# Turning a unit's row maxima by one fp16 matmul of pre-split parts instead of one fp32 matmul

## The chip, the cores and the metric

The kernel runs on one core of a Trainium2 chip. The metric is the device time of one execution in microseconds (us). The kernel before takes 2337.19 us, the median of three runs (2336.58 to 2337.27).

## The reference, cut to what matters

One transformer layer with attention and a feed-forward part side by side on the same normalised input: `x + attention(xn) + ffn(xn)`, for x of 2 x 1024 x 1024. What the change touches is the softmax of the attention:

```python
scores = jnp.einsum('bhqd,bhkd->bhqk', q, k) / np.sqrt(HEAD_DIM)   # 32 heads of 32 channels, 8 key heads
attn = jax.nn.softmax(scores, axis=-1)
out = jnp.einsum('bhqk,bhkd->bhqd', attn, v)
```

A softmax needs the maximum of each row of scores, which is taken off before the exponential.

## The kernel before, in words

The work has three stages: the projections to queries, keys and values (to about 236 us), attention (to about 1030 us), and the output projection with the feed-forward part. Every instruction is written out in Python, so each engine has one fixed order.

Attention goes over 32 units (one of 16 key-head and batch pairs, times two halves of the queries) of 16 steps each, 512 steps in all. In a unit there are 16 row tiles of 128 query rows. The scores are made twice. `row_scores` (L1448) makes them with queries on the partitions, into three PSUM banks in turn, and `row_max` (L1131) on VectorE reduces each bank of 512 columns to a maximum; this runs LEAD = 25 steps ahead. `key_scores` (L1501) makes them again with keys on the partitions, with two extra contraction rows that take off the row maximum; ScalarE takes the exponential (L809). `values` (L1515) multiplies by the values in fp32, GpSimd adds pairs of probability tiles (L649), and `pair_sums` (L1530) sums them by a matmul of ones in fp32.

TensorE runs `row_scores`, `key_scores`, `values` and `pair_sums` as sets of four matmuls, each with 32 columns of weights, in four column groups of the array (output partitions 0 to 31, 32 to 63, and so on). The set of an instruction raises its semaphore with its last matmul.

The maxima of a unit lie in `mxs` with the row's place on the partition and the tile on the column. They must become rows of `qst`, along the free dimension. The way there, for unit u + 1, in steps 6 to 8 of unit u:

- step 6: VectorE does the last `row_max` of unit u + 1, then `top_max` (L1135), which merges the two halves into `mtop` (128 x 16, fp32), and raises `top_ok`.
- step 7: TensorE, after its four score sets of this step, waits for `top_ok` and does `maxima_rows` (L1456): the fp32 matmul of `mtop` with the unit matrix into 16 partitions of bank 7. VectorE, after the two `row_max` of this step, does `split_rows` (L1140 and L1142): scale to a high fp16 part, then the rest as a low fp16 part, from PSUM, and raises `mrow_ok`.
- step 8: SyncE's queue sends the two parts to rows 96 and 97 of `qst` (`load_m`, L393). TensorE's first `pair_sums` of the unit (step 8) waits for `mrow_ok`, since it writes the same bank.

`row_scores` of set c waits in `max_ok` for the reduction of set c - 3, since there are three banks. On VectorE `settle()` makes the next instruction wait until the one before it has written.

Of the kernel before, what the change touches and what calls it, by code (L numbers as in the profile page):

```python
# [5 lines left out]
P = 128  # L6
# [14 lines left out]
MU = 16384.0  # L21
# [115 lines left out]
def layer_kernel(nc, x, wq, sq, wk, sk, wv, sv, wo, so, gw, gz, gs, uw, uz, us, dw, dz, ds, out, zscr, wscr, yscr, kscr, vscr, rscr):  # L137
    f32, f16, i32 = mybir.dt.float32, mybir.dt.float16, mybir.dt.int32
    ALU = mybir.AluOpType
    ACT = mybir.ActivationFunctionType  # L140
    AX = mybir.AxisListType.X
    add, sub, mult, amin, amax, iseq = ALU.add, ALU.subtract, ALU.mult, ALU.min, ALU.max, ALU.is_equal

    ctx = ExitStack()
    with ctx:
# [52 lines left out]
        zone_d = zone_b[:, 74 * 256:75 * 256]  # L198
        mxs = zone_d[:, 0:64].rearrange("p (n h c) -> p n h c", n=2, h=2)
        mtop = zone_d[:, 64:80]  # L200
        ones = zone_d[:, 80:112]
        dcp = zone_d[:, 112:144].rearrange("p (n c) -> p n c", n=2)

        woT = view(zone_b, 20, 4096, f16).rearrange("p (k c) -> p k c", k=FQ)
        woraw = [view(zone_b, kb, 1024) for kb in (0, 12, 44, 48, 52, 12, 44, 8)]
# [29 lines left out]
        id32 = sb("id32", [P, P])  # L235
        id16 = sb("id16", [P, P], f16)
        zone_c = sb("zone_c", [P, 768])
        bn = zone_c[:, 0:NX * 12].rearrange("p (n c) -> p n c", n=NX)
        mask = zone_c[:, 256:768]
        mrow = zone_c[0:16, 0:256].bitcast(f16).rearrange("p (n h c) -> p n h c", n=2, h=2)  # L240
        tab = zone_c[:, 0:IT * 16].rearrange("p (t m g) -> p t m g", t=IT, m=2)
        dtab = zone_c[:, IT * 16:IT * 24].rearrange("p (t o) -> p t o", t=IT)
        cmx = zone_c[:, IT * 24:IT * 26].rearrange("p (t m) -> p t m", t=IT)
# [19 lines left out]
        ps = ctx.enter_context(nc.psum_tensor("ps", [P, 8, 512], f32))  # L263
# [35 lines left out]
        s = {n: sem(n) for n in names}  # L299
# [40 lines left out]
        def _(sp):  # L340
# [49 lines left out]
            def load_m(u):  # L390
                sp.wait_ge(s["mrow_ok"], u + 1)
                for part in range(2):
                    sp.dma_start(qst[u % 3][96 + part:97 + part, :, :].rearrange("a h (q c) -> a (h q) c", q=4),  # L393
                                 mrow[:, u % 2, part, :]).then_inc(s[f"m_in{u % 3}"], 16)

            def store_kv(b):
                sp.dma_start(kscr[2 * b:2 * b + 2].rearrange("n h p c -> p n h c"), kz[:, 2 * b:2 * b + 2, :, :]
# [57 lines left out]
            for e in range(STEPS):  # L455
                u, k = e // 16, e % 16
# [509 lines left out]
        def _(dve):  # L966
            V = nc.vector
            ch = Tally(s["chain"])

            def settle():  # L970

                dve.wait_ge(s["chain"], ch.value())
# [159 lines left out]

            def top_max(u):
                dve.wait_ge(s["max_ok"], 32 * u + 32)
                V.tensor_reduce(mtop, mxs[:, u % 2, :, :].rearrange("p h c -> p c h"), AX, amax).then_inc(s["top_ok"], 1)  # L1135

            def split_rows(u):
                dve.wait_ge(s["m_pe"], u + 1)
                m = ps[0:16, 7, 0:P]
                ch.inc(V.tensor_scalar(mrow[:, u % 2, 0, :], m, -1.0 / MU, None, mult))  # L1140
                settle()
                V.scalar_tensor_tensor(mrow[:, u % 2, 1, :], m, -1.0 / MU, mrow[:, u % 2, 0, :], mult, sub).then_inc(s["mrow_ok"], 1)  # L1142

            def invert(u):
                dve.wait_ge(s[f"dc_in{u % 2}"], 64 * (u // 2 + 1))
# [3 lines left out]
            for c in range(NC):  # L1149
                i = 4 * (c + 1)  # L1150
                for p in range(12):
                    if c + 1 < NC:
                        if p == 0:
                            dve.wait_ge(s[f"x_in{c + 1}"], 64)
                            moments((i, i + 1))
                        elif p == 1:
                            if c == 0:
                                guard_output(0, 1)
                            moments((i + 2, i + 3))
                            statistics(c + 1)  # L1160
                        elif p == 2:
                            inverse_deviation(c + 1)
                            normalise((i, i + 1))
                        elif p == 3:
                            normalise((i + 2, i + 3))
                        elif c == 0 and p == 4:
                            low(i)
                        elif (7 if c == 0 else 6) <= p < 10:
                            low(i + p - 6)
                    for r in early_row(c, p, 0) + early_row(c, p, 1):  # L1170
                        row_max(r)
                        if r == 15:
                            top_max(0)
                    if (c, p) == (3, 9):
                        split_rows(0)
                    if (c, p) == (NC - 1, 11):
                        break
                    if (c, p) != (0, 1):
                        guard_output(c, p)
                    if (c, p) in ((0, 5), (0, 9)):  # L1180
                        place_weights(9 if p == 5 else 11)
                    if (c, p) == (0, 8):
                        negate_zeros()
                    if p >= 3:
                        tail(c, p - 1)
                if c + 1 < NC:
                    tail(c, 11)
# [106 lines left out]
            for e in range(STEPS):  # L1294
                u, k = e // 16, e % 16
                if e + LEAD < STEPS:
                    row_max(e + LEAD)
                if e == 0:
                    clamp_output(NC - 1, 11)
                elif e == 2:  # L1300
                    keep_numbers(NC - 1, 11)
                elif e in (5, 7):
                    tail(NC - 1, 10 + (e - 5) // 2)
                if k == 6 and u + 1 < UNITS:
                    top_max(u + 1)
                if k == 7 and u + 1 < UNITS:
                    split_rows(u + 1)
                if u == UNITS - 2 and k == 9:
                    table_sizes()
                if u == UNITS - 2 and k == 10:  # L1310
                    common_maxima()
                if k == 10 and u:
                    invert(u - 1)
                if u == UNITS - 2 and k == 11:
                    common_product()
                    ch.inc(V.tensor_scalar(fac[:, 2:3], cmr[:, 2:3], 256.0 * 1024.0 / QB, None, mult))
                    settle()
                if u == UNITS - 1:
                    if k == 2:
                        output_magnitude(0)  # L1320
                    elif k == 8:
                        output_magnitude(1)
                        output_scales(0)
                    elif k == 9:
                        evac_output_weights(0)
                    if by_vector(u, 1) and k % 4 == 3:
                        add_pair(u, k // 4, 1)
# [80 lines left out]
        def _(pe):  # L1408
            MM = nc.tensor.matmul
# [42 lines left out]
            def maxima_rows(u):  # L1452
                pe.wait_ge(s["top_ok"], u + 1)
                if u >= 2:
                    pe.wait_ge(s["evd_ok"], u - 1)
                MM(ps[0:16, 7, 0:P], mtop, id32[:], start=True, stop=True).then_inc(s["m_pe"], 1)  # L1456

            def project(c, p):
                n, b2, s2, f = 12 * c + p, c // 2, c % 2, channels(c, p)
# [145 lines left out]
            for e in range(STEPS):  # L1605
                u, k = e // 16, e % 16
# [104 lines left out]
            for hf in range(HALVES):  # L1711
                for j in range(PAIRS):
                    if hf == 1 and j in TURNS:
                        n = 2 * TURNS.index(j)
# [43 lines left out]
```

## Time and profile before

| what | value |
|---|---|
| median of the runs | 2337.19 us (2336.58 to 2337.27) |
| span of the profiled execution | 2335.8 us |
| TensorE busy, share of the span | 98% |
| VectorE / ScalarE / GpSimd busy | 77% / 68% / 42% |
| granted TensorE clock, mean | 0.997 of full speed |
| row maxima: `top_max` | 32 of 188 ns |
| row maxima: matmul | 64 halves of 272 ns |
| row maxima: `split_rows` | 32 of 269 ns and 32 of 279 ns |

The span goes from the first to the last instruction of the profiled execution; no separate time of that execution is given. Its span is 0.8 us under the fastest and 1.4 us under the median of the runs. Busy time of TensorE is modelled at the ends of matmuls, so starts of instructions say more than ends. In a timeline the columns are the start, the length, the engine, the line, the operation, the tiles and the count; several instructions of one line are merged, and brackets give idle time before them with what ended it. PEld is the weight load of TensorE.

### The profile page before, as it was taken

To read this page: it belongs to the slowest core of one execution; us is meant where nothing else is said; L and a number is where in the kernel's file an instruction comes from. 1 tells how busy PE (TensorE), PEld (TensorE's weight loads), DVE (VectorE), ACT (ScalarE), POOL (GpSimd) and SP (SyncE) were. 2 spreads that over 40 slices of the span, in tenths; PEclk is the share of its full clock that TensorE was granted. 3 is DMA by queue.
4 is the path that set the end of the run, shared out by engine and by line. 5 is a ranking of instruction groups with operands and counts; after the bars stand their busy time and mean duration, and the time that the engine had idled before them with its cause. 6 is when DMAs were issued, how large, how long until landed. Compare 5 with 4: busy or idle time off the path is not lost.

```text
span 2335.8 us, 44834 instructions
## 1 busy us (share of the span) xinstructions
PE 2284.4 (98%) x18443; PEld 1100.0 (47%) x18443; DVE 1809.7 (77%) x2313; ACT 1591.0 (68%) x2051; POOL 990.0 (42%) x559
## 2 busy tenths in 40 slices
PE   6999999999999999999999999999999999999998
PEld 3444455555555555534444444444444444444444
DVE  8878888888888888856677777777777777777777
ACT  6774788888888888872366666666665666666664
POOL 0450699999999999960022222210002222221000
PEclk9999999999999999999999999999999999999999
DMA  5891344444444444443111111121114111114111
GB/s 187 171 202 32 70 72 78 74 76 70 72 81 72 74 72 73 80 92 136 59 37 36 44 47 37 36 109 45 37 64 145 36 36 37 38 53 181 36 36 72
DMA packets 178305, 175.51 MB, mean 75 GB/s; under 512 B 87778, under 2 KB 127586, under 8 KB 178102
## 3 DMA queue, kind: packets, MB, share of 16 engines
q1 hardware_dynamic: 113590, 143.28, 19.5%
q0 software_dynamic: 64512, 29.37, 12.6%
q8 instruction: 146, 2.39, 0.4%
q14 instruction: 57, 0.47, 0.1%
HBM read 160.08 MB, written 65.45 MB: 97 GB/s over the span
## 4 chain that ended last, share of the span: by engine, by line
PE 90%; DVE 5%; ACT 2%; issue 1%; DMA 1%; SPq 0%; POOL 0%; DVEq 0%; ACTq 0%
PE ps L1676 33%; PE ps L1692 17%; PE ps L1448 9%; PE ps L1501 9%; PE ps L1515 9%; PE ps L1647 5%; PE ps L1530 4%; PE ps L1473 3%; DVE sm L977 1%; DVE zone L1112 1%; DVE zone L1016 1%; ACT zone L809 0%; ACT zone L741 0%; ACT zone L789 0%; DVE zone L1388 0%
## 5 line engine op out<-in xcount | busy, mean ns | idle before, releaser
L1676 PE MATMUL ps<-xT,zone 128*128 128x512 f16 x3584 | 774.6, 379 | 2.7 <-DVE zone L1388 2.7
L1131 DVE TENSOR_REDUCE zone<-ps 128x1 f32<-128x512 f32 x1024 | 639.1, 683 | 128.1 <-PE ps L1448 120.0
L809 ACT ACTIVATE zone<-ps,sm 128x512 f32<-128x512 f32 x1024 | 628.8, 693 | 115.3 <-PE ps L1501 110.9
L649 POOL TENSOR_TENSOR zone<-zone 128x1024 f32<-128x1024 f32 x252 | 619.1, 2543 | 123.9 <-ACT zone L809 70.0
L1365 DVE TENSOR_SCALAR ps<-ps,zone_c 128x1024 f32<-128x1024 f32 x392 | 506.7, 1293 | 160.5 <-PE ps L1676 158.5
L932 ACT ACTIVATE ps<-ps,zone_c 128x1024 f32<-128x1024 f32 x392 | 426.7, 1088 | 259.9 <-PE ps L1676 259.9
L1676 PEld LDWEIGHTS ps<-xT,zone 128*128 128x128 f16 x3584 | 350.3, 98 | 426.2 <-DVE zone L1388 4.2
L1448 PE MATMUL ps<-zone 96*32 96x512 f16 (+1 forms) x3946 | 437.3, 380 | 8.6 <-issue 3.6
L1501 PE MATMUL ps<-zone 98*32 98x512 f16 x4096 | 438.3, 381 | 4.5 <-ACT zone L809 4.2
L1692 PE MATMUL ps<-zone 128*128 128x512 f16 x1792 | 387.1, 379 | 0.0
L684 POOL CAST zone<-zone 128x1024 f16<-128x1024 f32 x56 | 58.1, 1037 | 692.2 <-DVE zone L1369 692.2
L1376 DVE TENSOR_SCALAR ps<-ps,zone_c 128x1024 f32<-128x1024 f32 x216 | 279.2, 1293 | 93.1 <-PE ps L1692 92.9
L946 ACT ACTIVATE ps<-ps,zone_c 128x1024 f32<-128x1024 f32 x216 | 235.1, 1088 | 137.8 <-PE ps L1692 137.8
L1515 PE MATMUL ps<-zone 128*32 128x512 f32 x2048 | 278.8, 594 | 0.7 <-ACT zone L809 0.7
L1692 PEld LDWEIGHTS ps<-zone 128*128 128x128 f16 x1792 | 175.3, 98 | 211.4
L1448 PEld LDWEIGHTS ps<-zone 96*32 96x32 f16 (+1 forms) x3946 | 145.8, 96 | 160.4 <-issue 65.7
L1501 PEld LDWEIGHTS ps<-zone 98*32 98x32 f16 x4096 | 145.5, 96 | 147.7 <-issue 71.7
L1473 PE MATMUL ps<-xT,zone 128*128 128x512 f16 x768 | 176.7, 384 | 1.0 <-DVE xT L1038 1.0
L692 POOL TENSOR_TENSOR xT<-xT,zone 128x1024 f32<-128x1024 f32 x8 | 18.7, 2358 | 361.8 <-ACT zone L951 361.8
L1530 PE MATMUL ps<-zone 128*32 128x512 f32 x1024 | 141.4, 595 | 0.0
L686 POOL TENSOR_TENSOR zone<-zone 128x1024 f16<-128x1024 f32 x56 | 119.1, 2127 | 4.5
L1473 PEld LDWEIGHTS ps<-xT,zone 128*128 128x128 f16 x768 | 74.9, 99 | 89.1 <-issue 5.9
(138 smaller groups left out, 1387.6 us busy)
## 6 DMA issues: line engine op xcount, KB each, us to landing
zone<-dequantised SPq DMA_DIRECT2D x84, 512.0 KB, 3.6
dequantised<-zero_points SPq DMA_DIRECT2D x56, 256.0 KB, 4.0
zone<-zone SPq DMA_DIRECT2D x384, 32.0 KB, 2.3
zone<-_attn_hidden_states_dram SPq DMA_DIRECT2D x16, 512.0 KB, 6.6
zone<-inverse_sums SPq DMA_DIRECT2D x128, 64.0 KB, 2.0
attention<-zone SPq DMA_DIRECT2D x32, 256.0 KB, 2.0
xT<-attention SPq DMA_DIRECT2D x4, 2048.0 KB, 12.2
dequantised<-zero_points POOLq DMA_DIRECT2D x28, 256.0 KB, 11.2
```

Of the source, the lines that this page charges most:

```text
L649: nc.gpsimd.tensor_tensor(duo[n % 3], prob[:, prob_slot(e), :], prob[:, prob_slot(e + 2), :], add).then_inc(s["sum_ok"], 1)
L809: A(prob[:, prob_slot(e), m % 2 * 512:(m % 2 + 1) * 512], ps[:, 3 + m % 3, :], ACT.Exp, scale=gam[:, 0:1]).then_inc(s["exp_ok"], 1)
L932: A(pair, pair, ACT.Copy, scale=tab[:, t, 0, g:g + 1]).then_inc(s["act_ok"], 1)
L1131: V.tensor_reduce(mxs[:, u % 2, half, i % 16:i % 16 + 1], ps[:, (2 * i + half) % 3, :], AX, amax).then_inc(s["max_ok"], 1)
L1365: V.tensor_scalar(pair, pair, tab[:, t, 1, g:g + 1], None, mult).then_inc(s["dve_ok"], 1)
L1376: V.tensor_scalar(pair, pair, dtab[:, it, o:o + 1], None, mult).then_inc(s["dve_ok"], 1)
L1448: last = MM(ps[a:a + wide, c % 3, :], qst[u % 3][0:96, i % 16 // 4, c0:c0 + wide], kst[0:96, u // 2 % 2, half * 512:(half + 1) * 512], sta ...
L1473: last = MM(ps[:, output_bank(n), :], wT[:, kt, f * P:(f + 1) * P], xT[:, b2, part, kt, s2 * 512:(s2 + 1) * 512], start=(kt == 0 and part ...
L1501: last = MM(ps[32 * b:32 * b + 32, 3 + m % 3, :], kst[0:98, u // 2 % 2, kt * P + 32 * b:kt * P + 32 * b + 32], qst[u % 3][0:98, 2 * hp + a ...
L1515: last = MM(ps[32 * h:32 * h + 32, 6, :], vst[:, u // 2 % 2, kt, :], prob[:, prob_slot(2 * kt + h // 2), h % 2 * 512:(h % 2 + 1) * 512], s ...
L1676: last = MM(ps[:, 4 * s2 + 2 * m + c, :], ring[:, buf, m * H + g * P:m * H + (g + 1) * P], xT[:, hf, part, g, c * 512:(c + 1) * 512], star ...
L1692: last = MM(ps[:, 4 * s2 + 2 * m + c, :], ring[:, k % RING, (it % 4) * 512 + o * P:(it % 4) * 512 + (o + 1) * P], hT[:, it, part, c * 512: ...
```

## The change

The scaling and the split move ahead of the turn. `top_max` now reduces, waits for the write, scales to the high part in fp16, waits again, and makes the low part, into `mparts` (128 x 32, fp16); only then it raises `top_ok`. It has a new wait for the earlier `maxima_rows`. The matmul takes the 32 columns of `mparts` as fp16 weights and the fp16 unit matrix. `split_rows` becomes `place_rows`, one copy of 32 partitions from PSUM to `mrow`. The two DMAs are as before, from other partitions.

```diff
+        mparts = zone_d[:, 144:160].bitcast(f16)
...
-        mrow = zone_c[0:16, 0:256].bitcast(f16).rearrange("p (n h c) -> p n h c", n=2, h=2)
+        mrow = zone_c[0:32, 0:128].bitcast(f16).rearrange("p (n c) -> p n c", n=2)
...
-                                 mrow[:, u % 2, part, :]).then_inc(s[f"m_in{u % 3}"], 16)
+                                 mrow[16 * part:16 * part + 16, u % 2, :]).then_inc(s[f"m_in{u % 3}"], 16)
...
             def top_max(u):
                 dve.wait_ge(s["max_ok"], 32 * u + 32)
-                V.tensor_reduce(mtop, mxs[:, u % 2, :, :].rearrange("p h c -> p c h"), AX, amax).then_inc(s["top_ok"], 1)
-
-            def split_rows(u):
+                ch.inc(V.tensor_reduce(mtop, mxs[:, u % 2, :, :].rearrange("p h c -> p c h"), AX, amax))
+                settle()
+                if u:
+                    dve.wait_ge(s["m_pe"], u)
+                ch.inc(V.tensor_scalar(mparts[:, 0:16], mtop, -1.0 / MU, None, mult))
+                settle()
+                V.scalar_tensor_tensor(mparts[:, 16:32], mtop, -1.0 / MU, mparts[:, 0:16], mult, sub).then_inc(s["top_ok"], 1)
+
+            def place_rows(u):
                 dve.wait_ge(s["m_pe"], u + 1)
-                m = ps[0:16, 7, 0:P]
-                ch.inc(V.tensor_scalar(mrow[:, u % 2, 0, :], m, -1.0 / MU, None, mult))
-                settle()
-                V.scalar_tensor_tensor(mrow[:, u % 2, 1, :], m, -1.0 / MU, mrow[:, u % 2, 0, :], mult, sub).then_inc(s["mrow_ok"], 1)
+                V.tensor_copy(mrow[:, u % 2, :], ps[0:32, 7, 0:P]).then_inc(s["mrow_ok"], 1)
...
-                MM(ps[0:16, 7, 0:P], mtop, id32[:], start=True, stop=True).then_inc(s["m_pe"], 1)
+                MM(ps[0:32, 7, 0:P], mparts, id16[:], start=True, stop=True).then_inc(s["m_pe"], 1)
```

`split_rows` is replaced by `place_rows` at both places where it was called.

## Rows read from the trace of the kernel before

**Rows 1.** The page, busy time of each engine (share of the span) and instructions

```profile
PE 2284.4 (98%) x18443; PEld 1100.0 (47%) x18443; DVE 1809.7 (77%) x2313; ACT 1591.0 (68%) x2051; POOL 990.0 (42%) x559
```

**Rows 2.** Groups of instructions by shape: busy us, mean ns | idle before, releaser

```profile
L1456 PE MATMUL ps<-id,zone 128*16 128x128 f32 x64 | 12.3, 272 | 0.2 <-DVE zone L1135 0.2
...
L1142 DVE SCALAR_TENSOR_TENSOR zone_c<-ps,zone_c 16x128 f16<-16x128 f32 x32 | 8.9, 279 | 1.1
...
L1140 DVE TENSOR_SCALAR zone_c<-ps 16x128 f16<-16x128 f32 x32 | 8.6, 269 | 0.5 <-PE ps L1456 0.5
...
L1135 DVE TENSOR_REDUCE zone<-zone 128x16 f32<-128x32 f32 x32 | 6.0, 188 | 1.1
```

**Rows 3.** Timeline of TensorE's matmuls around one turn, 472.9 to 479.6 us

```profile
472.95 0.41 PE L1448 MATMUL ps<-zone 96*32 96x512 f16 x4
...
476.46 0.38 PE L1456 MATMUL ps<-id,zone 128*16 128x128 f32 x2
...
476.90 0.38 PE L1501 MATMUL ps<-zone 98*32 98x512 f16 x1
477.12 0.38 PE L1448 MATMUL ps<-zone 96*32 96x512 f16 x1
477.19 0.53 PE L1501 MATMUL ps<-zone 98*32 98x512 f16 x4
...
478.27 1.16 PE L1530 MATMUL ps<-zone 128*32 128x512 f32 x8
479.13 0.52 PE L1448 MATMUL ps<-zone 96*32 96x512 f16 x4
```

**Rows 4.** Timeline of TensorE's weight loads around the same turn

```profile
476.84 0.15 PEld L1448 LDWEIGHTS ps<-zone 96*32 96x32 f16 x4
477.18 0.10 PEld L1501 LDWEIGHTS ps<-zone 98*32 98x32 f16 x4 [0.18 <-ACT zone L809]
...
478.11 0.41 PEld L1530 LDWEIGHTS ps<-zone 128*32 128x32 f32 x8 [0.45 <-issue]
```

**Rows 5.** Timeline of VectorE around the same turn, and the next turn's start

```profile
473.42 2.48 DVE L1131 TENSOR_REDUCE zone<-ps 128x1 f32<-128x512 f32 x4 [0.98 <-PE ps L1448]
475.94 0.19 DVE L1135 TENSOR_REDUCE zone<-zone 128x16 f32<-128x32 f32 x1
476.10 1.29 DVE L1131 TENSOR_REDUCE zone<-ps 128x1 f32<-128x512 f32 x2
...
477.81 1.27 DVE L1131 TENSOR_REDUCE zone<-ps 128x1 f32<-128x512 f32 x2
479.71 2.48 DVE L1131 TENSOR_REDUCE zone<-ps 128x1 f32<-128x512 f32 x4 [0.63 <-PE ps L1448]
...
500.48 0.19 DVE L1135 TENSOR_REDUCE zone<-zone 128x16 f32<-128x32 f32 x1
```

**Rows 6.** Timeline of VectorE in the statistics of the input, 96.3 to 99.8 us

```profile
96.95 0.16 DVE L993 TENSOR_SCALAR sm<-sm 128x4 f32<-128x4 f32 x1
97.03 0.16 DVE L994 TENSOR_SCALAR sm<-sm 128x4 f32<-128x4 f32 x1
...
98.89 0.16 DVE L1006 TENSOR_TENSOR sm<-sm 128x4 f32<-128x4 f32 x1
99.08 0.17 DVE L1008 TENSOR_SCALAR sm<-sm 128x4 f32<-128x4 f32 x1
```

**Rows 7.** Groups of instructions by shape: small VectorE instructions

```profile
L1209 DVE COPY zone_c<-ps 128x224 f32<-128x224 f32 x1 | 0.6, 578 | 0.0
...
L1254 DVE SCALAR_TENSOR_TENSOR zone_c<-sm,zone_c 128x28 f32<-128x28 f32 x1 | 0.2, 209 | 0.0
```

**Rows 8.** Timeline of VectorE at a turn with a stall behind it

```profile
600.62 1.29 DVE L1131 TENSOR_REDUCE zone<-ps 128x1 f32<-128x512 f32 x2 [1.80 <-PE ps L1448]
```

**Rows 9.** Timeline of weight loads at the turn that starts at 252.15 us

```profile
254.92 0.54 PEld L1530 LDWEIGHTS ps<-zone 128*32 128x32 f32 x8 [1.17 <-issue]
```

**Rows 10.** Timeline of weight loads at the last turn, 995.86 us

```profile
996.52 0.10 PEld L1501 LDWEIGHTS ps<-zone 98*32 98x32 f16 x4 [0.25 <-ACT zone L809]
```

More of the change, by code:

```diff
@@ L1174, in _ @@
                     if (c, p) == (3, 9):
-                        split_rows(0)
+                        place_rows(0)
                     if (c, p) == (NC - 1, 11):
@@ L1306, in _ @@
                 if k == 7 and u + 1 < UNITS:
-                    split_rows(u + 1)
+                    place_rows(u + 1)
                 if u == UNITS - 2 and k == 9:
```

## The prediction, made before the changed kernel was seen

> **What bounds the kernel now.** I read the page first. TensorE is busy 98% of the span, VectorE 77% [rows 1]; so a change pays or costs only where it moves TensorE. Then the groups of instructions by shape, for the price of what is removed [rows 2], and last the timelines of one turn of the maxima, engine by engine, because the change moves work of 0.1 us between engines and only an order in time tells who waits.
>
> The turn comes once a unit, and a unit takes 24.54 us (from 475.94 to 500.48) [rows 5]. On TensorE the four score matmuls of a set run in four column groups at once. The turn of 16 columns uses the first group alone: its two halves sit there for two steps of 0.11 us, while the other groups go on with the next set. So after the turn the first group is 0.22 us behind. One sees it in the rows: the four-matmul rows are 0.41 us long ahead of the turn and 0.52 us long after it, and the first group's last score matmul of the step stands alone at 477.12 [rows 3]. The late group counts: in the undisturbed place VectorE starts its reduction 0.47 us behind the first matmul of the set (472.95 to 473.42), after the turn 0.58 us (479.13 to 479.71) [rows 3, 5]. The semaphore comes when the slowest group is done. The other groups use their lead only to stand at the next wait for an exponential (477.18) [rows 4]. So the first group sets the pace of the unit, and it is where I count.
>
> **What is removed on TensorE.** Two halves of an fp32 matmul, 0.22 us of the first group per turn. One fp16 pass of 128 columns comes in; fp16 score matmuls of 512 columns follow each other in the first group after 0.22 us (476.90 to 477.12) [rows 3], so 128 columns are about 0.055 us. Gain: 0.165 us a turn, if nothing else waits.
>
> **What is added on VectorE, ahead of the signal.** `top_ok` used to fire at the end of one reduction of 0.19 us [rows 2]. Now two small instructions and two waits stand ahead of it. A small tensor-scalar takes 0.16 to 0.17 us on 4 columns [rows 6], say 0.175 on 16. The low part is a scalar-tensor-tensor: 0.209 us on 28 columns [rows 7], 0.279 on 128 columns from PSUM [rows 2]; at about 1 ns a column this leaves 0.16 to 0.20 on 16 columns, and I take 0.17, nearer to the shape that has its fp16 output. A waited start comes 0.035 us behind the end of the one before: 98.89 plus 0.16 to 99.08 [rows 6]. The chain is 0.19 + 0.035 + 0.175 + 0.035 + 0.17 = 0.605 us.
>
> VectorE starts the next, independent instruction 0.03 us ahead of the end of the last (475.94 plus 0.19 against 476.10) [rows 5]. The next `row_max` therefore starts at 475.94 + 0.605 - 0.03 = 476.515 instead of 476.10.
>
> **What waits for that.** `top_ok` itself arrives at about 476.60, and the weight load of the turn was wanted at 476.24. The turn's matmul starts at about 476.65 instead of 476.46, but is 0.165 shorter, so the set behind it starts at 476.70 against 476.68: this wait alone just eats the gain.
>
> Behind it is a second wait, and it is the one that decides. The second score set after the turn needs the bank that this `row_max` empties. Today it starts at 476.10, and the weights of that set load at 476.84, 0.74 us later [rows 4, 5], which is the reduction and the signal; the first group takes it at 477.12 anyway [rows 3]. With the `row_max` at 476.515 the release comes at 477.26 and the matmuls of all four groups start at 477.27 to 477.30. That is 0.15 to 0.18 us behind 477.12; a weight load that had to wait costs about 0.01 more. I take +0.165 us a turn for the group that sets the pace. From here to the next turn that group had nothing to spare: the exponentials and banks that it needs are there before it is ready for them (477.18 against 477.33, 0.22 behind 477.12), so the loss stays.
>
> Bounds of this step. Shortest: both instructions 0.155 and 0.16, the waits 0.03: the chain is 0.535, and the loss 0.09 us. Longest: 0.20 and 0.23, and 0.05 for the wait that now has two semaphores: 0.74 in all, and the loss 0.30 us.
>
> **What is taken off VectorE after the signal.** `split_rows` was 0.27 + 0.035 + 0.28 us [rows 2]; `place_rows` is one copy of 128 columns from PSUM, about 0.27. VectorE is 0.415 late into the step and gives 0.3 back, and it stood idle 0.63 us ahead of 479.71 [rows 5], which covers the rest; without this cover the next reductions would be 0.1 us late. `mrow_ok` came at 477.89 (0.19 + 0.28 ahead of the `row_max` at 477.81, which overlaps by 0.07). It now comes when two `row_max` of 0.605 us and the copy are done: 476.515 + 1.21 + 0.27 = 478.00. The pair sums wait for it; their weights load 0.22 us after it today (478.11) [rows 4]. With 478.22 that is well ahead of the new start of 478.58 (478.27 today [rows 3], plus 0.31 for the three groups that lose their lead). The two DMAs of step 8 start 0.1 us later, and the unit's key scores need them six steps, some 9 us, later. SyncE's queue behind them next wants step 11. POOL waits for the pair sums, and moves with TensorE. The new wait for the last unit's turn is 24 us old when it is asked.
>
> **The sum over the turns.** Of the 31 turns in the loop, 24 look like the one shown, with the `row_max` 0.16 us behind `top_max` and the turn's matmul at 0.52.
> - 24 x 0.165 = +4.0 us.
> - Four turns have a stall of TensorE on the queries and keys right ahead (VectorE idle 1.53, 1.80, 0.67 and 1.88 us, at 351.72, 598.63, 796.96 and 895.81); one of them is shown [rows 8]. There VectorE has finished the chain before TensorE asks, and the shorter matmul counts: 4 x -0.16 = -0.6 us.
> - The turn at 674.09 has a short stall (`row_max` 0.31 behind); gain and loss cancel: 0.
> - The turn at 252.15 lies in a stretch where VectorE is the late one and TensorE's pair sums wait for `mrow_ok` (1.17 us idle) [rows 9]. There the whole growth of VectorE's work counts: 0.415 + 0.27 - 0.585 = +0.1, with a margin +0.2.
> - The turn at 995.86 has no `row_max` behind it, and the next exponential ends TensorE's wait anyway [rows 10]: 0.
> - The turn of unit 0 is in the projections, long after its maxima are ready: -0.16.
>
> Together +3.4 us. The profiled span of 2335.8 becomes 2339.2; the median of the runs lies 1.4 above the span, so 2340.6 us, +0.15%.
>
> **A rule weighed.** The rows have two small instructions start 0.08 us apart without a wait (96.95, 97.03) and 0.19 us apart with one (98.89, 99.08) [rows 6], and the chain of 0.605 us is made of the second kind. The Trainium skill, "VectorE: DVE Perf Modes", section "The DRAIN you can't avoid", says that an operation waits for the pipeline to empty anyway and that the semaphore costs nothing extra. By that rule the two kinds would be alike; the rows differ by 0.11 us. What a cheap wait would give is the third rival.
>
> **The rivals.**
> - *TensorE keeps its gain.* If the chain on VectorE were hidden, each turn would save 0.165 us: 31 x -0.165 = -5.1, 2332.1 us. It decides when the `row_max` behind the chain starts by 476.20, a chain of at most 0.29 us; up to 476.36 there is still some gain. For it speaks that TensorE is at 98% and this is pure TensorE work. Against it, three small instructions with waits between them in the rows never come near 0.29.
> - *The two cancel.* Only the wait for `top_ok` counts and the bank's release does not bind, because the groups take the set in another order than I read: 24 x 0, less 0.8 in the special turns, 2336.4 us. For it: the release (476.84) lies close to where the set would load anyway, and may be dispatch and not the semaphore.
> - *The waits are cheap.* If a wait on the instruction just ahead cost no more than the 0.08 us of an unwaited start, the chain would be 0.08 + 0.08 + 0.19 = 0.35 us, the `row_max` would start at 476.26 and the second set at 477.01: 24 x -0.11 - 0.8 = -3.4, 2333.8 us. The skill's rule named above speaks for it; 32 waited pairs of the old split, 0.31 us apart for 0.27 us of work, speak against it.
> - *The pair sums wait for the copy.* If `place_rows` is slow, `mrow_ok` binds too. A copy from PSUM took 0.578 us for 224 columns [rows 7]; at that rate 128 columns would be 0.33 to 0.39. Then `mrow_ok` comes at 478.12, still 0.2 us short of binding. It takes a copy above 0.6 us; then the loss would be some 0.4 us a turn, 24 x 0.4 = +9.6, 2346.8 us.
> - *The stalls on the queries move.* The four stalls and the short one make about 7 us in all. They hang on how transfers lie to each other, and a unit that is 0.2 us longer could shift them by up to their sum either way: from 2333.6 to 2347.6 with the rest as forecast. They hold in part for the other cases too.
>
> **How the numbers follow.** What a measurement of this kernel can tell from no change is about 0.2%, 4.7 us, so from 2332.5 to 2341.9 us is the same. My forecast, the bank's release, gets 0.64. Its own range is 24 x 0.09 - 0.8 = +1.4 to 24 x 0.30 - 0.6 = +6.6, 2338.6 to 2343.8 us; 0.40 of it lies within 0.2% and 0.24 above. TensorE keeps its gain: 0.08, faster. The two cancel: 0.11, same. The waits are cheap: 0.05, same. The pair sums wait: 0.08, slower. Moved stalls: 0.04, half faster, half slower. Faster is 0.10, same 0.56, slower 0.34. The range goes from the cheap waits to the far end of the forecast with a little for the stalls, 2333.6 to 2344.5 us; what is left out, 0.20, is the kept gain, the pair sums and the moved stalls.
>
> **What the changed profile would show.** In a turn like the one shown: `row_max` 0.58 us behind the reduction of `top_max` (0.16 today); the turn's matmul at 0.70 (0.52); four-matmul rows of 0.41 us on both sides of the turn, since no group is behind; the second score set at 1.33 to 1.36 us in all groups (1.18 in the first today), with its weight load released by VectorE; a unit of 24.70 us (24.54). In the turns with a stall, that stretch is 0.16 us shorter. I am wrong if the `row_max` is later or earlier than 0.55 to 0.71, if the second score set doesn't follow it by 0.75, or if the unit's length doesn't follow that set.

## The result, and the profile after

The changed kernel takes 2440.13 us (median of four runs, 2438.49 to 2445.97) against 2336.89 (four runs, 2336.35 to 2337.27) of the kernel before on the same chip: a ratio of 1.0444, 95% interval 1.0431 to 1.0457. That is 103 us slower where the prediction said 3.4. The profiled execution has a span of 2436.7 us against 2335.8.

The page of the changed kernel, busy time by engine, and the end of its chain by engine:

```profile
PE 2300.7 (94%) x18411; PEld 1021.0 (42%) x18411; DVE 1900.2 (78%) x2345; ACT 1595.2 (65%) x2051; POOL 987.6 (41%) x559
PE 83%; DVE 12%; ACT 2%; issue 1%; DMA 0%; SPq 0%; DVEq 0%; POOL 0%; ACTq 0%
```

VectorE has 90.5 us more of busy time (1809.7 before [rows 1]). The groups by shape say which instructions hold it; behind the bar are the busy time, the mean ns of one, and the idle time ahead with its releaser:

```profile
L1142 DVE SCALAR_TENSOR_TENSOR zone<-zone 128x16 f16<-128x16 f32 x32 | 53.7, 1677 | 1.1
L1140 DVE TENSOR_SCALAR zone<-zone 128x16 f16<-128x16 f32 x32 | 47.9, 1498 | 1.1
L1146 DVE CAST zone_c<-ps 32x128 f16<-32x128 f32 x32 | 8.6, 269 | 0.3 <-PE ps L1460 0.3
L1136 DVE TENSOR_REDUCE zone<-zone 128x16 f32<-128x32 f32 x32 | 6.0, 187 | 1.1
L1460 PE MATMUL ps<-id,zone 128*32 128x128 f16 x32 | 7.5, 235 | 84.2 <-DVE zone L1142 84.2
```

The two new instructions on 16 columns were priced at 0.175 and 0.17 us. They take 1.50 and 1.68 us in the mean, 101.6 us together, of which 32 x 0.345 = 11 was foreseen. The reduction (L1136) and the copy (L1146) cost what was foreseen. TensorE waits 84.2 us for them at the turn (L1460), in 30 of the 32 turns.

One plain turn, VectorE, GpSimd and TensorE in the timelines (start, length, instruction; it is the tenth turn, the one of [rows 3, 5] is the eleventh):

```profile
471.72 0.19 DVE L1136 TENSOR_REDUCE zone<-zone 128x16 f32<-128x32 f32 x1
471.94 0.82 DVE L1140 TENSOR_SCALAR zone<-zone 128x16 f16<-128x16 f32 x1
472.80 2.27 DVE L1142 SCALAR_TENSOR_TENSOR zone<-zone 128x16 f16<-128x16 f32 x1
474.98 1.27 DVE L1132 TENSOR_REDUCE zone<-ps 128x1 f32<-128x512 f32 x2
```

```profile
471.46 1.27 POOL L654 TENSOR_TENSOR zone<-zone 128x512 f32<-128x512 f32 x1
472.69 2.33 POOL L650 TENSOR_TENSOR zone<-zone 128x1024 f32<-128x1024 f32 x1
```

```profile
472.60 0.40 PE L1505 MATMUL ps<-zone 98*32 98x512 f16 x4
475.12 0.23 PE L1460 MATMUL ps<-id,zone 128*32 128x128 f16 x1 [2.11 <-DVE zone L1142]
475.12 0.44 PE L1452 MATMUL ps<-zone 96*32 96x512 f16 x4
```

```profile
475.72 0.10 PEld L1452 LDWEIGHTS ps<-zone 96*32 96x32 f16 x4 [0.43 <-DVE zone L1132]
```

Read the ends. The tensor-scalar starts while GpSimd's divide (L654, a product with the inverted sums) runs and ends at 472.76, 0.03 us behind the divide's end at 472.73. The scalar-tensor-tensor starts 0.11 us into GpSimd's pair add (L650) and ends at 475.07, 0.05 behind the add's end at 475.02 on these rounded numbers. The end of each is set by an engine with which it shares no data. The first wait makes the second: it brings VectorE to the start of the next add, and so into its whole length. `row_max` (L1132), which empties the bank for TensorE, starts 3.26 us behind the merge, where it was 0.16 [rows 5] and 0.575 was forecast. The second score set loads its weights 0.74 us after that, at 475.72, released by it. From merge to merge the unit is 27.34 us long (471.72 to 499.06), 24.54 before.

In 23 of the 32 turns it is so. In the turns of units 0 and 1 GpSimd stands idle, and both instructions take what was forecast:

```profile
213.20 0.17 DVE L1140 TENSOR_SCALAR zone<-zone 128x16 f16<-128x16 f32 x1
213.41 0.18 DVE L1142 SCALAR_TENSOR_TENSOR zone<-zone 128x16 f16<-128x16 f32 x1
```

In the seven others GpSimd is issuing a DMA of weights (L622) when the merge is done. There the tensor-scalar alone takes 2.7 to 4.5 us and the second instruction 0.17; VectorE, then GpSimd, then TensorE:

```profile
526.61 4.49 DVE L1140 TENSOR_SCALAR zone<-zone 128x16 f16<-128x16 f32 x1
531.13 0.17 DVE L1142 SCALAR_TENSOR_TENSOR zone<-zone 128x16 f16<-128x16 f32 x1
```

```profile
526.10 1.39 POOL L622 DMA_DIRECT2D dequantised<-in_L_ffn_gate_w_dram  x1
526.89 1.87 POOL L654 TENSOR_TENSOR zone<-zone 128x512 f32<-128x512 f32 x1
528.12 2.93 POOL L650 TENSOR_TENSOR zone<-zone 128x1024 f32<-128x1024 f32 x1
```

```profile
531.37 0.23 PE L1460 MATMUL ps<-id,zone 128*32 128x128 f16 x1 [4.28 <-DVE zone L1142]
```

The tensor-scalar ends at 531.10, 0.05 behind the end of the add at 531.05, having waited through the divide and the add, although both started after it. A second cost hangs on these long waits. The windows of the turn and of the time behind it (length, busy time of PE, PEld, DVE, ACT and POOL, then the granted clock of TensorE, the DMA share and GB/s):

```profile
526.60:533.00 6.40, 2.12 (x33) 0.68 (x25) 6.36 (x6) 2.24 (x4) 4.46 (x3) 0.92 0.62 46
533.00:540.00 7.00, 7.00 (x88) 2.42 (x84) 4.63 (x9) 4.02 (x7) 3.82 (x2) 0.82 0.13 40
```

TensorE, busy 2.12 us of 6.40, is then busy without a gap at a granted clock of 0.82 in the mean, so for a part of that time at the lower of its two levels (1.2 GHz). From 200 to 1100 us, windows of 10 us put together lose 17 us of full clock after the change and 1.7 before; some of that falls where TensorE stands idle anyway.

### The profile page after: what moved, and what is told of

Read it like the earlier page. It is cut to its first block, busy times and chain, and to the rows that moved or that the text cites. A ratio compares the mean times of both kernels' runs of the same rounds, so it can differ in the third digit from the quotient of the medians.

```text
span 2436.7 us, 44833 instructions
## 1 busy us (share of the span) xinstructions
PE 2300.7 (94%) x18411; PEld 1021.0 (42%) x18411; DVE 1900.2 (78%) x2345; ACT 1595.2 (65%) x2051; POOL 987.6 (41%) x559
## 4 chain that ended last, share of the span: by engine, by line
PE 83%; DVE 12%; ACT 2%; issue 1%; DMA 0%; SPq 0%; DVEq 0%; POOL 0%; ACTq 0%
PE ps L1680 32%; PE ps L1696 16%; PE ps L1519 8%; PE ps L1452 8%; PE ps L1505 7%; PE ps L1534 5%; PE ps L1651 5%; DVE zone L1132 3%; DVE zone L1142 2%; PE ps L1477 2%; DVE zone L1140 2%; DVE zone L1113 1%; DVE sm L978 1%; ACT zone L810 1%; DVE zone L1017 0%
## 5 line engine op out<-in xcount | busy, mean ns | idle before, releaser
L1132 DVE TENSOR_REDUCE zone<-ps 128x1 f32<-128x512 f32 x1024 | 638.5, 681 | 135.0 <-PE ps L1452 126.9
L650 POOL TENSOR_TENSOR zone<-zone 128x1024 f32<-128x1024 f32 x252 | 615.2, 2491 | 226.5 <-PE ps L1534 154.9
L1680 PEld LDWEIGHTS ps<-xT,zone 128*128 128x128 f16 x3584 | 350.4, 98 | 426.1 <-DVE zone L1392 4.2
L1452 PE MATMUL ps<-zone 96*32 96x512 f16 (+1 forms) x3946 | 408.4, 384 | 8.0 <-issue 4.6
L1505 PE MATMUL ps<-zone 98*32 98x512 f16 x4096 | 409.6, 384 | 4.3 <-ACT zone L810 4.1
L1696 PE MATMUL ps<-zone 128*128 128x512 f16 x1792 | 387.1, 379 | 0.0
L1519 PE MATMUL ps<-zone 128*32 128x512 f32 x2048 | 274.0, 607 | 0.7 <-ACT zone L810 0.7
L1452 PEld LDWEIGHTS ps<-zone 96*32 96x32 f16 (+1 forms) x3946 | 114.4, 96 | 195.5 <-DVE zone L1132 82.8
L1505 PEld LDWEIGHTS ps<-zone 98*32 98x32 f16 x4096 | 117.4, 97 | 169.5 <-issue 55.2
L1534 PE MATMUL ps<-zone 128*32 128x512 f32 x1024 | 137.9, 612 | 0.2 <-issue 0.2
L1651 PE MATMUL ps<-zone 128*128 128x512 f16 x512 | 112.2, 379 | 0.0
```

The source lines that it names most:

```text
L650: nc.gpsimd.tensor_tensor(duo[n % 3], prob[:, prob_slot(e), :], prob[:, prob_slot(e + 2), :], add).then_inc(s["sum_ok"], 1)
L1132: V.tensor_reduce(mxs[:, u % 2, half, i % 16:i % 16 + 1], ps[:, (2 * i + half) % 3, :], AX, amax).then_inc(s["max_ok"], 1)
L1452: last = MM(ps[a:a + wide, c % 3, :], qst[u % 3][0:96, i % 16 // 4, c0:c0 + wide], kst[0:96, u // 2 % 2, half * 512:(half + 1) * 512], sta ...
L1505: last = MM(ps[32 * b:32 * b + 32, 3 + m % 3, :], kst[0:98, u // 2 % 2, kt * P + 32 * b:kt * P + 32 * b + 32], qst[u % 3][0:98, 2 * hp + a ...
L1519: last = MM(ps[32 * h:32 * h + 32, 6, :], vst[:, u // 2 % 2, kt, :], prob[:, prob_slot(2 * kt + h // 2), h % 2 * 512:(h % 2 + 1) * 512], s ...
L1534: last = MM(ps[32 * h:32 * h + 32, 7, :], ones, duo[(n + h // 2) % 3][:, h % 2 * 512:(h % 2 + 1) * 512], start=(j == 0), stop=(j == 3))
```

## The experiments

Two theories stood at first. **The port**: VectorE and GpSimd share an access to SBUF; an instruction of VectorE that needs it waits for the whole running instruction of GpSimd. **The chain**: two instructions that each wait for the one before are dear in themselves, or the wait for the last unit's turn (`m_pe`) is. The trace of the changed kernel speaks for the port by the ends of the instructions, but only a change of source, form or neighbour shows it. The runs of the kernel before beside the experiments had medians of 2337.34 us (e1 to e4), 2336.93 (e5 to e7) and 2338.09 (e8); each ratio is against its own. e2, e3 and e4 have two runs each, the others ten or eleven.

**e1: the same chain, read from PSUM.** The merged maxima go to 16 spare columns of the turn's PSUM bank. Both instructions keep their shape, their order and their waits; only their source is elsewhere. The merge gets one more wait, since the bank has to be free.

```diff
+                top = ps[:, 7, 256:272] if u else mtop
+                if u >= 2:
+                    dve.wait_ge(s["evd_ok"], u - 1)
-                ch.inc(V.tensor_reduce(mtop, mxs[:, u % 2, :, :].rearrange("p h c -> p c h"), AX, amax))
+                ch.inc(V.tensor_reduce(top, mxs[:, u % 2, :, :].rearrange("p h c -> p c h"), AX, amax))
...
-                ch.inc(V.tensor_scalar(mparts[:, 0:16], mtop, -1.0 / MU, None, mult))
+                ch.inc(V.tensor_scalar(mparts[:, 0:16], top, -1.0 / MU, None, mult))
```

(and the same `top` in the instruction after it)

> The changed kernel, but for all units except the first the merged maxima are written to 16 free columns of PSUM bank 7, and the scaling and the low part read them from there. The port theory (a VectorE instruction that needs the second SBUF read interface waits until GpSimd's instruction ends): neither reads two SBUF tensors or one in a two-port mode now, so both take 0.15 to 0.25 us and the chain 0.6 us; the unit falls from 27.33 to about 24.70 us and the time to 2340 us, the sum of the prediction. The rival (small instructions that write fp16 to SBUF behind a wait are slow by themselves): the outputs and waits are the same, so the two stay at 0.82 and 2.27 us and the time at 2440.

Measured: 2340.91 us (2336.31 to 2345.36), ratio 1.0008 [0.9999, 1.0018]. Of the 103 us 3.6 are left by the medians, 1.9 by the ratio. The profiled execution is the slowest of the eleven; a plain turn is read in it. The groups, and one turn on VectorE and on the weight loads:

```profile
L1143 DVE TENSOR_SCALAR zone<-ps 128x16 f16<-128x16 f32 x31 | 5.4, 175 | 1.1
L1145 DVE SCALAR_TENSOR_TENSOR zone<-ps,zone 128x16 f16<-128x16 f32 x31 | 5.4, 174 | 1.1
```

```profile
479.91 0.20 DVE L1139 TENSOR_REDUCE ps<-zone 128x16 f32<-128x32 f32 x1
480.14 0.17 DVE L1143 TENSOR_SCALAR zone<-ps 128x16 f16<-128x16 f32 x1
480.35 0.17 DVE L1145 SCALAR_TENSOR_TENSOR zone<-ps,zone 128x16 f16<-128x16 f32 x1
480.45 1.28 DVE L1132 TENSOR_REDUCE zone<-ps 128x1 f32<-128x512 f32 x2
```

```profile
481.18 0.10 PEld L1455 LDWEIGHTS ps<-zone 96*32 96x32 f16 x4 [0.43 <-DVE zone L1132]
```

The chain with all its waits is cheap, 0.175 and 0.174 us for the instructions: the chain theory falls. A scalar-tensor-tensor with one input in PSUM and one in SBUF isn't held up either. This run is also the one that shows what the prediction's own mechanism does once the port is out of the way; the section below comes back to it.

**e3, e4, e5: one extra instruction in the kernel before.** Each puts one instruction behind the merge whose result nobody reads and for which nobody waits: a tensor-scalar with one SBUF input (e3), a scalar-tensor-tensor with two (e4), and as a control a reciprocal with one (e5).

```diff
                 V.tensor_reduce(mtop, mxs[:, u % 2, :, :].rearrange("p h c -> p c h"), AX, amax).then_inc(s["top_ok"], 1)
+                ch.inc(V.tensor_scalar(spare, mxs[:, u % 2, 0, :], -1.0 / MU, None, mult))
```

(e4: `V.scalar_tensor_tensor(spare, mxs[:, u % 2, 0, :], -1.0 / MU, mxs[:, u % 2, 1, :], mult, sub)`; e5: `V.reciprocal(spare, mxs[:, u % 2, 0, :])`, with an fp32 output)

> The kernel before, with one extra tensor-scalar of VectorE (128 x 16, fp32 to fp16, SBUF to SBUF) behind the merge of the maxima, whose output nobody reads. Port theory: it starts while GpSimd's 1.27 us product runs and ends with it, some 0.9 us later, so the row_max behind it is late by 0.9 and the unit by 0.6 to 0.7 us; where GpSimd issues a DMA at that point, more: 2335 + 20 to 30 us. The rival (it is the waits between dependent instructions): it takes 0.17 us, 2337 us.

> The kernel before, with one extra scalar-tensor-tensor (two SBUF inputs of 128 x 16, fp16 out) behind the merge of the maxima, whose output nobody reads. Port theory: as the extra tensor-scalar, 0.9 us each, 2337 + 20 to 30 us: either form blocks, and its own speed doesn't matter. The rival (it is the waits): 0.17 us, 2337 us.

> The kernel before, with one extra reciprocal (one SBUF input of 128 x 16, fp32) behind the merge of the maxima, whose output nobody reads; the control to the extra tensor-scalar and scalar-tensor-tensor. Port theory: it has one input and no two-port mode, so it takes its 0.24 us in each turn; the row_max starts 0.2 us later, the second score set is released at 1.10 us behind the merge, before the first column group wants it at 1.18, and the time stays at 2337. If any extra instruction at this place costs a lot, it is 2350 or more.

Measured: e3 2387.62 us, 1.0214 [1.0195, 1.0233]; e4 2386.38 us, 1.0209 [1.0190, 1.0227]; e5 2337.42 us, 1.0002 [0.9993, 1.0011]. The group of the extra instruction in e3, in e4 and in e5:

```profile
L1138 DVE TENSOR_SCALAR zone<-zone 128x16 f16<-128x16 f32 x32 | 51.3, 1603 | 0.0
```

```profile
L1138 DVE SCALAR_TENSOR_TENSOR zone<-zone 128x16 f16<-128x16 f32 x32 | 51.3, 1602 | 0.0
```

```profile
L1138 DVE RECIPROCAL zone<-zone 128x16 f32<-128x16 f32 x32 | 7.8, 243 | 0.0
```

One instruction of 16 columns that computes nothing of use costs 50 us, with no wait on a semaphore ahead of it and none behind; a reciprocal in the same place, longer by itself, costs nothing that can be measured. One input is as bad as two. A plain turn of e3, VectorE and GpSimd:

```profile
486.92 0.96 DVE L1138 TENSOR_SCALAR zone<-zone 128x16 f16<-128x16 f32 x1
487.80 0.68 DVE L1133 TENSOR_REDUCE zone<-ps 128x1 f32<-128x512 f32 x1
```

```profile
486.57 1.28 POOL L655 TENSOR_TENSOR zone<-zone 128x512 f32<-128x512 f32 x1
487.81 2.36 POOL L651 TENSOR_TENSOR zone<-zone 128x1024 f32<-128x1024 f32 x1
```

The tensor-scalar ends at 487.88, 0.03 behind the divide; the reduction behind it starts at 487.80 and runs undisturbed beside GpSimd's next add. That reduction, the reciprocal and the PSUM sources of e1 are free; what is held up is the tensor-scalar and the two-input form between SBUF and SBUF. The size was a miss: 20 to 30 us were expected and 50 came. In the plain turns the unit grows by 0.52 us, 23 x 0.52 = 12 us; in seven turns the instruction waits 2.8 to 4.65 us, and the seven units behind them, 2.4 to 7.0 us longer than before, carry the rest.

**e2: GpSimd's add in two halves.** If VectorE waits for the end of the running instruction, shorter instructions should shorten the wait.

```diff
-                nc.gpsimd.tensor_tensor(duo[n % 3], prob[:, prob_slot(e), :], prob[:, prob_slot(e + 2), :], add).then_inc(s["sum_ok"], 1)
+                for a in (0, 512):
+                    ins = nc.gpsimd.tensor_tensor(duo[n % 3][:, a:a + 512], prob[:, prob_slot(e), a:a + 512], prob[:, prob_slot(e + 2), a:a + 512], add)
+                ins.then_inc(s["sum_ok"], 1)
```

> The changed kernel, with each of GpSimd's pair adds (128 x 1024) as two instructions of 512 columns. Port theory: the low part waits for at most one half, so 2.27 us falls to about 1.1, the scaling stays at 0.82, the unit falls by about 1.1 to 26.2 us and the time to some 2405 us, though GpSimd does more work. If VectorE can't get in between two GpSimd instructions, nothing changes or it gets worse. The rival (slow by themselves): 2.27 us stay, 2440 us or more.

Measured: 2484.13 us, 1.0627 [1.0599, 1.0655], some 43 us slower than the changed kernel by the two ratios: a miss. One turn, VectorE and then GpSimd:

```profile
393.09 3.60 DVE L1142 TENSOR_SCALAR zone<-zone 128x16 f16<-128x16 f32 x1
396.72 0.17 DVE L1144 SCALAR_TENSOR_TENSOR zone<-zone 128x16 f16<-128x16 f32 x1
```

```profile
392.74 1.48 POOL L656 TENSOR_TENSOR zone<-zone 128x512 f32<-128x512 f32 x1
393.96 2.68 POOL L651 TENSOR_TENSOR zone<-zone 128x512 f32<-128x512 f32 x2
```

VectorE waits through the divide and both halves, to 0.05 us behind the end at 396.64. Only in nine turns does it get in behind the divide (0.94 to 0.97 us), and then its second instruction takes 1.19, one half of an add. So "it waits for the running instruction" is too kind a rule: between instructions that GpSimd has queued back to back VectorE is often passed over. Which of the gaps it gets, these runs don't say.

**e8: GpSimd's add made short.** The changed kernel, SBUF sources and all, with a pair add of 128 columns in place of 1024. It leaves out seven eighths of those sums, so what it returns is no attention; only its times are read.

```diff
-                nc.gpsimd.tensor_tensor(duo[n % 3], prob[:, prob_slot(e), :], prob[:, prob_slot(e + 2), :], add).then_inc(s["sum_ok"], 1)
+                if n < 3:
+                    nc.gpsimd.memset(duo[n % 3], 8.0).then_inc(s["sum_ok"], 1)
+                else:
+                    nc.gpsimd.tensor_tensor(duo[n % 3][:, 0:128], prob[:, prob_slot(e), 0:128], prob[:, prob_slot(e + 2), 0:128], add).then_inc(s["sum_ok"], 1)
```

> The changed kernel, with VectorE's and TensorE's instructions as they are, but GpSimd's pair adds on 128 of 1024 columns (the rest of the sums is a constant, so the softmax's denominators are left out in part; the 28 adds that VectorE or the set-up does otherwise stay in number). Port theory: GpSimd is through with its work of a step long before the merge of step 6, so the port is free, the scaling and the low part take 0.17 us each although they read SBUF, and the time is that of the variant that reads PSUM, 2341 us. If the SBUF source is slow by itself, or the small fp16 writes are, the two stay long and the time at some 2440 us.

Measured: 2334.54 us, 0.9988 [0.9979, 0.9998]. The three groups:

```profile
L653 POOL TENSOR_TENSOR zone<-zone 128x128 f32<-128x128 f32 x249 | 128.5, 516 | 526.1 <-PE ps L1537 476.9 <-ACT zone L813 49.1
L1143 DVE TENSOR_SCALAR zone<-zone 128x16 f16<-128x16 f32 x32 | 6.7, 210 | 1.1
L1145 DVE SCALAR_TENSOR_TENSOR zone<-zone 128x16 f16<-128x16 f32 x32 | 6.4, 199 | 1.1
```

Not one line of VectorE's or TensorE's work differs from the changed kernel, and the 103 us are gone with GpSimd's long adds. This closes the case from GpSimd's side, as e1 did from VectorE's. The total isn't a clean measure of the rest, since GpSimd has less to do in every step; the durations are: 0.210 and 0.199 us, 0.17 in most turns. Its plain units are 24.61 us long, like those of e1 (24.62).

It also answers what a DMA issue of GpSimd does by itself. In seven turns the tensor-scalar starts while one runs, and takes 0.17 us; here one of them, VectorE and then GpSimd:

```profile
423.60 0.17 DVE L1143 TENSOR_SCALAR zone<-zone 128x16 f16<-128x16 f32 x1
```

```profile
422.83 1.40 POOL L622 DMA_DIRECT2D dequantised<-in_L_ffn_up_w_dram  x1
```

**e6 and e7: two versions that keep the gain on TensorE.** e6 is the kernel before with the merge writing bf16 and one bf16 matmul by a bf16 identity; the maximum only shifts the exponential, and both parts are still split from the rounded value, so the shift cancels. Nothing is added on VectorE; GpSimd makes the identity once, at the start.

```diff
-                V.tensor_reduce(mtop, mxs[:, u % 2, :, :].rearrange("p h c -> p c h"), AX, amax).then_inc(s["top_ok"], 1)
+                with nc.allow_low_precision(reason="any shift near the maximum serves"):
+                    V.tensor_reduce(rounded, mxs[:, u % 2, :, :].rearrange("p h c -> p c h"), AX, amax).then_inc(s["top_ok"], 1)
...
-                MM(ps[0:16, 7, 0:P], mtop, id32[:], start=True, stop=True).then_inc(s["m_pe"], 1)
+                MM(ps[0:16, 7, 0:P], rounded, idb, start=True, stop=True).then_inc(s["m_pe"], 1)
```

> The kernel before, with the matmul part of the change alone: the merge writes its maxima rounded to bf16, one bf16 matmul of 16 columns turns them, and the split stays behind it, read from PSUM. The shift that is taken off is then the rounded maximum, which cancels in the softmax. Nothing is added ahead of the signal. If the first column group sets the pace, 31 turns save 0.165 us each: -5 us, 2332. If the turn is hidden in the slack of the other groups: 2337.

e7 is e1 with one reduction of step 7 between the merge and the split, so that the bank is emptied first, and the turn moved behind it, ahead of the values of step 8.

```diff
                 for half in range(2):
+                    if half and between:
+                        between()
...
+                turn = (lambda: split_maxima(u + 1)) if k == 7 and u + 1 < UNITS else None
                 if e + LEAD < STEPS:
-                    row_max(e + LEAD)
+                    row_max(e + LEAD, turn)
...
+                    if k == 8 and u + 1 < UNITS:
+                        maxima_rows(u + 1)
...
-                elif k == 7 and u + 1 < UNITS:
-                    maxima_rows(u + 1)
```

> The variant with the merged maxima in PSUM, in another order: VectorE does the first reduction of step 7 between the merge and the two instructions of the split, and TensorE does the turn in step 8, ahead of the fp32 values matmul. The chain is then 1.1 us behind the merge and is wanted 1.5 us behind it; the reduction whose bank the second set needs starts where it does in the kernel before. Port theory and the prediction's count of the first column group: the gain of the short matmul stays, 31 x -0.165 = -5 us, 2332. If the turn blocks the column groups ahead of the fp32 sets, or if mrow_ok is late for the pair sums, it is 2337 or more.

Measured: e6 2333.03 us (2329.50 to 2334.90), 0.9982 [0.9973, 0.9991]; e7 2333.52 us (2332.71 to 2336.79), 0.9987 [0.9979, 0.9996]. Their units are 24.40 and 24.42 us long in the median (24.54 before). Both are faster than the kernel before, by 4 and 3 us, and neither interval reaches 1; the prediction gave 31 x 0.165 = 5.1 us to a kernel whose chain is hidden, which the interval of e6 (2.1 to 6.3 us) holds and that of e7 (0.9 to 4.9) just misses. In e6 the turn is one matmul:

```profile
L1465 PE MATMUL ps<-zone 128*16 128x128 bf16 x32 | 7.0, 220 | 0.2 <-DVE zone L1142 0.2
```

## Why the prediction was wrong, step by step

**What is removed on TensorE: right.** 0.165 us a turn was counted; the unit of e6, where nothing else changes in the turn, is 0.14 shorter in the median.

**What is added on VectorE, ahead of the signal: this step failed.** "A small tensor-scalar takes 0.16 to 0.17 us on 4 columns [rows 6], say 0.175 on 16", and for the second "I take 0.17". As prices of the instructions these are right: 0.175 and 0.174 in e1. As prices in this place they are not: 1.50 and 1.68 us in the mean. The durations were taken from the statistics of the input [rows 6] and from other places, with only the shape and the form compared, and not what GpSimd was doing at the time. The bounds had the same hole: 0.23 us was the longest, and none of the five rivals had a resource shared between VectorE and GpSimd. (The bounds are also added up wrongly: their terms give chains of 0.565 and 0.705 us, not 0.535 and 0.74. Against the 3.35 us that the chain now takes this is nothing.)

The trace of before had what was needed. GpSimd around the turn of [rows 5]:

```profile
475.68 1.28 POOL L653 TENSOR_TENSOR zone<-zone 128x512 f32<-128x512 f32 x1
476.92 2.37 POOL L649 TENSOR_TENSOR zone<-zone 128x1024 f32<-128x1024 f32 x1
```

And VectorE beside GpSimd's first adds, where two instructions with all inputs in SBUF take three times their usual time (774 ns is the mean of 48 for L1112, 781 of 40 for L1122):

```profile
242.33 2.32 DVE L1112 COPY_PREDICATED zone<-zone_c,zone 128x512 f32<-128x512 int32 x1
248.57 2.35 DVE L1122 SCALAR_TENSOR_TENSOR zone<-zone,sm 128x512 f16<-128x512 f32 x1 [0.26 <-ACT zone L789]
```

```profile
241.67 5.16 POOL L649 TENSOR_TENSOR zone<-zone 128x1024 f32<-128x1024 f32 x2 [64.49 <-ACT zone L809]
248.00 2.36 POOL L649 TENSOR_TENSOR zone<-zone 128x1024 f32<-128x1024 f32 x1 [1.18 <-ACT zone L809]
```

The second of them ends 0.56 us behind the end of GpSimd's add (250.92 against 250.36), and its usual length is 0.74 us: it did most of its work only when the add was through.

Whoever reads these rows so can work out the cost. The tensor-scalar, ready at 476.17, ends 0.03 behind the divide, at 476.99. The second starts at 477.03, inside the add, and ends at 479.32. `row_max` starts at 479.29, the bank is released 0.74 us later at 480.03, and the first group, which wanted it at 477.12, is 2.9 us late. Measured are +2.80 us a unit. The old split never met this, since it reads PSUM, and neither do the reductions.

The Trainium skill states the rule, in "SBUF — State Buffer", section "Who interferes with whom": the pair of ports that VectorE and GpSimd share is an exclusive lock, which a VectorE instruction takes in a two-port mode (tensor-scalar and copies can enter it) or, against a GpSimd instruction that reads SBUF, with two inputs in SBUF; and whoever comes second waits for the whole of the other's instruction. The runs agree in each form that they tried: tensor-scalar (e3) and two inputs (e4) are held up, reciprocal (e5), reductions and PSUM sources (e1) are not. They differ in one thing: by the page whoever issues first gets the pair, so the wait is for one instruction, and in e2 it goes over three, two of which started after VectorE's.

**The sum.** The two instructions are longer by 23 x (0.82 + 2.27 - 0.345) = 63 us in the plain turns. In the seven with a DMA issue the first takes 28.7 us in all, 27.4 more than foreseen. Together 90.5 us, and 94 with the 3.4 forecast; the spans differ by 100.9. The last 7 us are of the size of what the lower clock takes behind the long waits. The wait alone makes a unit of 24.54 us plus the start of `row_max` behind the merge, plus 0.74 us to the release, less the 1.18 at which the first group took the set before. For the unit at 471.72 that is 27.36 (27.34 measured). For the one at 277.63, whose long wait is the shortest (2.72 us) and whose clock stayed full, it is 27.17 (27.17). For the one at 526.38 it is 28.94, and 30.64 were measured: 1.7 more, with a granted clock of 0.94 in the mean. The five other units behind long waits are 1.6 to 2.1 us over in the same way. That the clock is the whole cause was not tested, since no run holds it up.

**What waits for that: the mechanism was right, its size a little too large.** e1 is the forecast case, and the marks of the prediction can be read there. `row_max` starts 0.54 us behind the merge (0.575 forecast), the turn's matmul 0.67 (0.70), and the second score set loads its weights, released by VectorE as foretold, 1.27 us behind it (1.33, and 1.18 before). The unit has 24.62 us (24.70). So half of the 0.165 us a turn came, 0.08 to 0.09, at the low bound of 0.09. The total is in keeping with that: +1.9 us by the ratio, where 24 x 0.08 less 0.6 gives +1.3; its interval, -0.2 to +4.2 us, holds the +3.4 too, and zero. In the changed kernel the same wait sets the pace, with a `row_max` that is far later (the weight load at 475.72).

**What is taken off after the signal: right.** `place_rows` takes 0.269 us (0.27). The weight load of the pair sums follows it by 0.23 us in a plain turn, as it followed the split before, but their matmuls start only 0.57 us behind it (0.39 before), so it holds nobody up. The turn at 252.67 is the exception that the prediction made of it: there the matmuls start 0.26 us behind the copy, and TensorE was idle for 0.17.

**The rule weighed.** Waited instructions start 0.21 to 0.23 us apart in e1 for 0.17 to 0.20 us of work, against 0.10 from the last waited one to the unwaited `row_max`. So the wait costs about 0.11 us here too, and the runs stay against the rule of the Trainium skill, "VectorE: DVE Perf Modes", section "The DRAIN you can't avoid", that the semaphore costs nothing extra; the page gives it for eight copies of 13.88 us in all, and only small instructions were read here. The waits are some 0.2 us of the 3.1 by which `row_max` is now later.

**The rivals.** That TensorE keeps its gain (2332.1 us) is what happens, in the main, once the chain is truly off the path: e6 and e7. Against "the two cancel" and "the waits are cheap" stands e1: VectorE does release the second set, at 1.27 us, and `row_max` starts 0.54 us behind the merge, where cheap waits would give 0.32. The pair sums' wait and moved stalls did not make the 103 us.

## What to carry to other kernels

Before a small VectorE instruction is put ahead of a signal, look at its sources and at GpSimd at that moment: a tensor-scalar from SBUF to SBUF, or one with two inputs in SBUF, was done here only when GpSimd's running instruction was, or a later one, whatever its own size. Take a duration for a sum only from a row in which the other engines do what they will do in the new place; the price from an idle neighbourhood was off by a factor of nine. A source in PSUM or a form that stays out of the shared port gives the time back, and better still was the change that adds nothing ahead of the signal, e6.

## What the runs showed of the hardware that was not expected

- VectorE can be passed over by GpSimd instructions that follow each other: 3.6 us through three in e2, up to 4.65 us through two in e3. In plain turns of the changed kernel it always gets in between the divide and the next add. And GpSimd can be held up too: at 242.33 in the kernel before VectorE came in between two adds, and the two took 5.16 us together instead of 2 x 2.37. Left open is what decides.
- All the long waits of the changed kernel and of e3 begin while GpSimd issues a DMA (0.8 to 1.4 us). The issue by itself holds nothing up: in seven turns of e8 the tensor-scalar started within one and took 0.17 us, and in four of e2, the first at 458.60 us, the scalar-tensor-tensor did. What the long waits have besides are long GpSimd instructions queued right behind the issue; why VectorE is passed over by those is open.
- The engine that pays need not be one of the two that collide: TensorE waited 84.2 us at the turn for VectorE's signal, and after a long wait ran 7 us at a granted clock of 0.82 in the mean.
